# A fused gate and attention kernel: the opening written out as one straight program per engine, up to the fourth pair's turn

## The chip, the cores and the metric

The kernel runs on one core of a Trainium2 chip. The metric is the device time of one execution in microseconds (us), the median of three runs. The profile is one more execution, in which every instruction leaves a record.

## What is computed

The input x is 32 images of 64 channels of 16x16 points. Two blocks follow each other.

```
y  = mean of x over points; y = conv1d(y, w_c) over channels       # channel gate
yc = sigmoid(x * y)
sa = sigmoid(conv5x5([mean over channels of yc, max over channels of yc], w_s))   # spatial gate
x  = yc * sa + x
xn = group_norm(x, 32 groups of 2 channels) * gn_w + gn_b
q, k, v = split(qkv_w @ xn + qkv_b)         # 4 heads of 16 channels, 256 points
out = x + proj_w @ (softmax(q.T k / 4) v) + proj_b
```

All is float32. The scores are computed from q and k that are each split into three bfloat16 parts.

## The kernel before

**Pairs, units, turns.** Two images make a pair (2 x 64 channels on 128 partitions), so there are 16 pairs. A pair has eight units, one for each head of each image. The work is staged: in turn k, pair k+5 gets its spatial gate and its group statistics, k+4 is normalised (`xn`), k+3 gets queries and keys (`qk`, TensorE) and their split into three parts (GpSimd: `rest`, middle part, last part), k+2 has those parts stacked into the tiles `qs` and `ks` through DRAM, k+1 has its scores (`s`, L768) and the row maxima (`negmax`, VectorE L608), and k (from the fifth unit on) and k-1 have transposed scores (`st`, L780), exponentials (ScalarE L448) and products with the values (L794). The maxima come back into the transposed scores as one more row of `qs`: a transpose (L847), a copy (L436) and a DMA (`qs<-maxrow`, L282). Each engine runs through `turn(k, ...)`, and semaphores order the engines among each other. A wait stops all that stands behind it on its engine.

**Opening, loop and end.** Turns -5 to 2 are written out by `peeled`, turns 3 to 10 are a hardware loop over laps of four turns, turns 11 to 17 are written out again. What only the opening has (sums, maps and gates of all images, pair 0's own split) stands in between units, in dictionaries `aside` and in `beginning`:

```
peeled(range(-AHEAD, LOOP_FROM))
aside = {(-3, 6): split_0, (-2, 6): lambda: channel_gate(4), (-1, 3): lambda: channel_gate(5), (0, 3): rest_of_gates}
```

**The sync queue (SP).** Nearly all DMAs are issued by SP, in the order of its program. In a turn it issues the loads of part 0 of pair k+2, the row of maxima of pair k, the other loads of pair k+2, and the writes of the parts of pair k+3. The spatial gates of pairs 4 to 15 go through DRAM as well: `gate_write` stores a chunk, `gate_read` reads it back, spread over the channels (two DMAs for each group of four pairs, `gate<-gate_dram`). Groups 2 and 3 are read behind turns 0 and 1:

```
aside = {(-2, 1): lambda: gate_read(sp, 1), (0, 2): lambda: gate_read(sp, 2), (1, 2): lambda: gate_read(sp, 3)}
```

**Pair 0** doesn't go through DRAM: `direct` copies its parts in 12 DMAs, seven from SP and five from ScalarE's queue.

Of the kernel before, what the change touches and what calls it, by code (L numbers as in the profile page):

```python
# [16 lines left out]
F32 = mybir.dt.float32  # L17
# [5 lines left out]
P = 128  # L23
# [10 lines left out]
TERMS = ((0, 0), (1, 0), (2, 0), (0, 1), (1, 1), (0, 2))  # L34
# [3 lines left out]
BLOCKS = ((0, 1), (1, 2), (2, 4), (4, 8), (8, 12), (12, 16))  # L38
# [6 lines left out]
MAP_BANK = (0, 1, 2, 0, 2, 2, 2, 2, 2)  # L45
# [9 lines left out]
def program(nc, x, vecs, w_all, select, consts, out):  # L55
    ctx = ExitStack()
    with ctx:
# [6 lines left out]
        quad = ctx.enter_context(nc.psum_tensor("quad", [P, 4, 512], F32))  # L64
        bank = [quad[:, i, :] for i in range(4)] + [ctx.enter_context(nc.psum_tensor(f"bank{i}", [P, 512], F32)) for i in range(4, 8)]
# [79 lines left out]
        gate_in = [sem(f"gate_in{g}") for g in range(GROUPS)]  # L145
# [8 lines left out]
        split_step = sem("split_step")  # L154
        parts_out, stack_in = [sem(f"parts_out{i}") for i in range(3)], [sem(f"stack_in{r}") for r in range(RING)]
# [22 lines left out]
        AHEAD, BEHIND = 5, 2  # L178
        LOOP_FROM, LOOP_TO = 3, 11

        def stands_in(aside, k, u):

            if isinstance(k, int) and (k, u) in aside:
                aside[k, u]()

        def pipeline(eng, turn):
# [6 lines left out]
            peeled(range(-AHEAD, LOOP_FROM))  # L193
# [6 lines left out]
        def gate_write(eng, chunk, first, last, row):  # L200

            eng.wait_ge(gate_ready, chunk + 3)
            eng.dma_start(gate_dram[first:last, :], gate_s[row:row + last - first, chunk, :]).then_inc(gate_out[chunk], 16)

        def gate_read(eng, g):
            eng.wait_ge(gate_out[0 if g == 1 else 1], 16)
            for a in range(2):
                src = gate_dram[2 * g * GROUP:2 * (g + 1) * GROUP, :].rearrange("(q i) n -> i q n", i=2)[a]
                eng.dma_start(gate[C * a:C * (a + 1), g * GROUP:(g + 1) * GROUP, :],
                              src.unsqueeze(0).broadcast_to([C, GROUP, N])).then_inc(gate_in[g], 16)  # L210

# [728 lines left out]
```

## Time and profile before

| | |
|---|---|
| median of 3 runs | 183.79 us (183.75 to 183.99) |
| profiled execution: time, span of its records | 184.61 us, 182.6 us |
| TensorE busy | 163.2 us, 89% of the span |
| VectorE, ScalarE, GpSimd busy | 136.5, 121.6, 106.3 us |
| mean granted TensorE clock | 0.947 of full |

The span is from the first record to the last; times "at" something are counted from its start. PE is TensorE (PEld its weight loads), DVE VectorE, ACT ScalarE, POOL GpSimd; SPq and ACTq are the DMAs that SP and ScalarE issue. A row of a timeline has start, duration, engine, line, operation, output<-input and a count; in brackets stands how long the engine was idle before it and what ended that.

### The profile page before, as it was taken

What the parts mean: (1) busy time and instruction counts of PE and PEld (TensorE: products, weight loads), DVE (VectorE), ACT (ScalarE), POOL (GpSimd) and SP (SyncE); (2) the same over time, 40 slices, a digit from 0 to 9 for tenths busy, and PEclk for the clock granted to TensorE, in tenths of its full rate; (3) what the DMA queues carried; (4) which work ended last, traced back from release to release, by engine and by line L of the source; (5) the groups of instructions that cost most, each with busy time, mean ns of one, the idle gap of its engine ahead of it and who ended that gap; (6) DMA issues with size and microseconds to landing.
All of it is one profiled execution on the core that took longest, in us unless ns stands there. A gap on an engine that the chain in (4) does not pass through costs nothing.

```text
span 182.6 us, 4762 instructions
## 1 busy us (share of the span) xinstructions
PE 163.2 (89%) x1508; PEld 107.3 (59%) x1511; DVE 136.5 (75%) x280; ACT 121.6 (67%) x254; POOL 106.3 (58%) x206
## 2 busy tenths in 40 slices
PE   6988829999685999999999999999999999998791
PEld 3778428776451857666675766767575754553220
DVE  1567663677661889898998989899897978876433
ACT  3552343455682679887987988798797965758730
POOL 8926072681977267888888778888858350101110
PEclk9999955899997899999999999999999999999967
DMA  5940487516189544555464564564646465110001
GB/s 138 336 149 0 100 105 224 153 59 176 63 196 232 151 134 130 173 164 187 130 204 148 162 201 148 169 183 163 173 132 186 139 203 148 36 32 30 29 0 57
DMA packets 19296, 25.31 MB, mean 139 GB/s; under 512 B 3568, under 2 KB 16400, under 8 KB 19280
## 3 DMA queue, kind: packets, MB, share of 16 engines
q1 hardware_dynamic: 18560, 24.62, 46.2%
q10 hardware_dynamic: 720, 0.48, 1.6%
q8 instruction: 9, 0.15, 0.4%
q14 instruction: 7, 0.06, 0.1%
HBM read 16.22 MB, written 8.02 MB: 133 GB/s over the span
## 4 chain that ended last, share of the span: by engine, by line
PE 77%; DVE 5%; ACT 4%; POOL 4%; issue 3%; DMA 2%; ACTq 2%; SPq 2%; POOLq 0%
PE bank L794 17%; PE quad L768 16%; PE quad L780 14%; PE bank L805 7%; PE bank L824 5%; PE quad L662 5%; PE bank L815 4%; PE bank L640 2%; DMA qs<-maxrow 2%; PE bank L674 2%; ACT pt L448 2%; ACTq L217 2%; DVE negmax L608 2%; PE bank L838 1%; POOL rest L355 1%
## 5 line engine op out<-in xcount | busy, mean ns | idle before, releaser
L608 DVE TENSOR_REDUCE negmax<-quad 128x2 bf16<-128x512 f32 x128 | 83.4, 678 | 21.1 <-PE quad L768 19.4
L448 ACT ACTIVATE pt<-quad 128x512 f32<-128x512 f32 x128 | 72.8, 594 | 23.2 <-PE quad L780 23.2
L780 PE MATMUL quad<-qs,ks 97*128 97x256 bf16 x256 | 49.4, 275 | 6.7 <-ACT pt L448 3.5
L768 PE MATMUL quad<-ks,qs 96*128 96x256 bf16 x256 | 50.5, 279 | 1.2 <-DVE negmax L608 0.4
L794 PE MATMUL bank<-pt,vs 128*32 128x256 f32 x512 | 35.8, 399 | 0.0
L768 PEld LDWEIGHTS quad<-ks,qs 96*128 96x128 bf16 x256 | 21.9, 101 | 22.3 <-DVE negmax L608 13.1
L780 PEld LDWEIGHTS quad<-qs,ks 97*128 97x128 bf16 x256 | 23.8, 98 | 14.7 <-ACT pt L448 6.3
L328 POOL TENSOR_TENSOR xall<-yo,xall 128x256 f32 (+1 forms) x15 | 11.0, 731 | 31.7 <-ACT yo L472 31.7
L794 PEld LDWEIGHTS bank<-pt,vs 128*32 128x32 f32 x512 | 15.1, 112 | 12.9 <-ACT pt L448 3.3
L355 POOL TENSOR_TENSOR rest<-z,parts 128x512 f32<-128x512 f32 x15 | 17.3, 1156 | 8.0 <-issue 5.9
L805 PE MATMUL bank<-xn,wall 128*128 128x256 f32 x64 | 19.9, 397 | 0.0
L370 POOL TENSOR_TENSOR parts<-rest,parts 128x512 bf16<-128x512 f32 x15 | 17.3, 1155 | 1.5
L456 ACT ACTIVATE parts<-bank,vec 128x512 bf16<-128x512 f32 x16 | 10.8, 675 | 10.4 <-PE bank L805 7.3
L575 DVE STREAM_TRANSPOSE otok<-bank 128x512 f32<-128x512 f32 (+1 forms) x17 | 11.5, 677 | 5.9 <-PE bank L794 5.9
L440 ACT ACTIVATE xn<-xall,gnb,gna 128x256 f32<-128x256 f32 (+1 forms) x16 | 9.6, 599 | 7.4 <-POOL gnb L365 7.2
L341 POOL TENSOR_TENSOR sq<-gmv 128x1 f32<-128x1 f32 x16 | 3.1, 194 | 17.5 <-DVE gmv L561 17.4
L586 DVE STREAM_TRANSPOSE onorm<-otok 128x512 f32<-128x512 f32 (+1 forms) x17 | 11.6, 680 | 1.2 <-PE bank L824 0.6
L824 PE MATMUL bank<-onorm,wall 128*32 128x256 f32 x128 | 10.7, 406 | 1.6 <-DVE onorm L586 1.6
L662 PE MATMUL quad<-con,ycall 128*128 128x130 f32 x64 | 10.8, 321 | 0.1
L805 PEld LDWEIGHTS bank<-xn,wall 128*128 128x128 f32 x64 | 10.0, 194 | 1.1 <-issue 0.6
L335 POOL TENSOR_TENSOR ycall<-ycall,gate (+1 forms) x12 | 8.7, 726 | 3.3 <-DMA gate<-gate_dram 3.3
L815 PE MATMUL bank<-wall,xn 128*128 128x128 f32 x64 | 10.4, 287 | 0.0
(66 smaller groups left out, 207.7 us busy)
## 6 DMA issues: line engine op xcount, KB each, us to landing
parts_dram<-parts SPq DMA_DIRECT2D x45, 128.0 KB, 2.0
ks<-parts_dram SPq DMA_DIRECT2D x15, 192.0 KB, 3.0
qs<-parts_dram SPq DMA_DIRECT2D x15, 192.0 KB, 3.2
out<-xall SPq DMA_DIRECT2D x16, 128.0 KB, 2.1
qs<-parts_dram SPq DMA_DIRECT2D x15, 128.0 KB, 2.7
ks<-parts_dram SPq DMA_DIRECT2D x15, 128.0 KB, 2.8
xall<-x SPq DMA_DIRECT2D x3, 512.0 KB, 6.0
gate<-gate_dram SPq DMA_DIRECT2D x6, 256.0 KB, 4.1
```

The lines of the kernel that those rows point to most:

```text
L355: nc.gpsimd.tensor_tensor(rest[:, :], z32[:, :], parts[:, r, 0, :], ALU.subtract).then_inc(split_step, 1)
L370: nc.gpsimd.tensor_tensor(parts[:, r, 2, :], rest[:, :], parts[:, r, 1, :], ALU.subtract).then_inc(split_step, 1)
L448: nc.scalar.activation(pt[:, (u + LEAD) % UNITS, :, :].rearrange("p t n -> p (t n)"), st_bank[u % 2][:, :], ACT.Exp, scale=SCALE).then_inc ...
L586: op = nc.vector.transpose(onorm[:, cols], o_tok[:, blocks, :].rearrange("p b c -> p (b c)"))
L608: nc.vector.tensor_reduce(negmax[:, slot(1), column:column + TILES], s_bank[u % 2][:, :].rearrange("p (t n) -> p t n", t=TILES), AX.X, ALU ...
L662: mm = pe.matmul(bank[MAP_BANK[i] + p - first][:, t * (P + 2):(t + 1) * (P + 2)], ycall[:, p, t * P:(t + 1) * P], con[:, C_IDENT:C_TOEP], ...
L768: mm = pe.matmul(s_bank[u % 2][:, t * N:(t + 1) * N], qs[0:KQ, slot(1), h, a, t * P:(t + 1) * P], ks[0:KQ, slot(1), h, a, :], start=True, ...
L780: mm = pe.matmul(st_bank[u % 2][:, t * N:(t + 1) * N], ks[0:KQ + 1, slot(d), h, a, t * P:(t + 1) * P], qs[0:KQ + 1, slot(d), h, a, :], sta ...
L794: mm = pe.matmul(o_bank[32 * h:32 * h + 32, a * N:(a + 1) * N], vs[:, slot(-1), t, a, h, :], pt[:, HEADS * a + h, t, :], start=(t == 0), s ...
L805: mm = pe.matmul(z_bank[:, a * N:(a + 1) * N], w_qk[a], xn[:, slot(d), :], start=True, stop=True)
L815: mm = pe.matmul(v_psum[:, t * P:(t + 1) * P], xn[:, slot(1), t * P:(t + 1) * P], w_v, start=True, stop=True)
L824: mm = pe.matmul(y_psum[C * a + j:C * a + j + 32, :], w_p[:, j:j + 32], onorm[:, a * N:(a + 1) * N], start=True, stop=True)
```

## The change

The turns -5 to 2 are gone from `pipeline`. In their place every engine has a list of calls and waits, in an order that a search over the operations' graph gave. Turn 3 and all later ones are as before. Besides the order:

- x comes in seven blocks and not six; PSUM banks are dealt out anew (z_bank is bank 7, y_psum bank 5).
- Pair 0's queries and keys, their split and its copies go in halves (one image each). Part 0 of its keys goes through DRAM, and there are nine direct copies and one stack in place of 12 direct copies.
- Pair 0's group variance, scale and shift are computed on VectorE, except for the power.
- The gates of pairs 8 to 15 are no sigmoid on ScalarE any more, but an exponential there (`late_gates`), then a sum and a reciprocal on VectorE (`late_gate_sum`, `late_gate_reciprocal`). They come behind the switch to the exponential table. The spatial convolutions go in three chunks and not two.
- The rows of maxima of pairs 0, 1 and 2 are issued by ScalarE; from pair 3 on SP does it.

```diff
-BLOCKS = ((0, 1), (1, 2), (2, 4), (4, 8), (8, 12), (12, 16))
+BLOCKS = ((0, 1), (1, 2), (2, 4), (4, 6), (6, 8), (8, 12), (12, 16))
...
-            peeled(range(-AHEAD, LOOP_FROM))
...
+            sp.wait_ge(split_step, 12)
+            part_write(2, 0)
+            sp.wait_ge(gate_ready, 5)
+            late_gate_write(sp)
+            sp.wait_ge(parts_out[1], 64)
+            stack(qs, 0, 3, 2, 0)
+            stack(ks, 1, 3, 2, 0, part=1)
+            sp.wait_ge(parts_out[2], 64)
+            stack(qs, 0, 0, 3, 0)
+            stack(ks, 1, 5, 1, 0, part=2)
+            sp.wait_ge(gate_out[1], 16)
+            gate_read(sp, 2, 0)
+            gate_read(sp, 2, 1)
+            sp.wait_ge(late_gate_in, 32)
+            gate_read(sp, 3, 0)
+            gate_read(sp, 3, 1)
+            sp.wait_ge(p1_ready, 5)
+            part_write(0, 1)
+            sp.wait_ge(split_step, 14)
+            part_write(1, 1)
+            sp.wait_ge(split_step, 15)
+            part_write(2, 1)
...
+            def late_gates():
+                nc.scalar.activation(gate_s[0:4 * GROUP, 0, :], chunk_bank[2][0:4 * GROUP, 0:N], ACT.Exp, scale=-1.0).then_inc(dexp_ready, 1)
...
+            exponentials(3)
+            late_gates()
...
+            dve.wait_ge(s_ready, 26)
+            maximum(3, 1)
+            dve.wait_ge(gs_ready, 7)
+            group_moments()
+            norm_reciprocal()
+            dve.wait_ge(gn_stat, 15)
+            aggregate()
+            late_gate_reciprocal()
+            maximum(3, 2)
```

In the calls, `maximum(p, u)`, `scores(p, u)` and `scores_t(p, u)` are unit u of pair p. The wait for `parts_out[2]` at 64 is for the last part of pair 4.

**SP, from the writes of pair 4's parts to the loop.** Before, from turn 1: the last three lines of a turn, the reads of group 3, and turn 2 with pair 4's loads (`qs<-parts_dram`, `ks<-parts_dram`) around pair 2's row of maxima:

```order
L261 DMA parts_dram<-parts 128x512 x3
L209 DMA gate<-gate_dram 64x4x256 x2
L257 DMA ks<-parts_dram 48x1x2048
L257 DMA qs<-parts_dram 16x2048
L282 DMA qs<-maxrow 1x16x128
L257 DMA qs<-parts_dram 32x1x2048
L257 DMA ks<-parts_dram 32x1x2048
L257 DMA qs<-parts_dram 48x1x2048
L257 DMA ks<-parts_dram 16x2048
L261 DMA parts_dram<-parts 128x512 x3
```

The changed kernel at the same place; the three writes are pair 5's parts, and the first two loads behind the branch and the row of maxima are turn 3's (pair 5, pair 3):

```order
L251 DMA parts_dram<-parts 128x512
L201 DMA gate_dram<-gate_s 16x256
L248 DMA qs<-parts_dram 32x1x2048
L248 DMA ks<-parts_dram 32x1x2048
L248 DMA qs<-parts_dram 48x1x2048
L248 DMA ks<-parts_dram 16x2048
L205 DMA gate<-gate_dram 64x4x256 x4
L251 DMA parts_dram<-parts 128x512 x3
L191 UNCONDITIONAL_BRANCH
L191 ISA
L248 DMA ks<-parts_dram 48x1x2048
L248 DMA qs<-parts_dram 16x2048
```

All four reads of late gates moved behind the loads of pair 4 and ahead of the writes of pair 5's parts, which before stood two turns behind the first of these reads; the row of maxima of pair 3 is the next DMA behind the last row shown.

**VectorE, the first pair.** Before, from the first block's sums to the first pair's statistics (`ysum<-xall` are channel sums, `maps` the channel maximum and mean, `ycall<-ycall,gate` the first gating):

```order
L482 TENSOR_REDUCE ysum<-xall 128x2
L490 TENSOR_REDUCE maps<-quad 128x2x2
L493 COPY maps<-quad 128x2x2
L490 TENSOR_REDUCE maps<-quad 128x2x2
L493 COPY maps<-quad 128x2x2
L482 TENSOR_REDUCE ysum<-xall 128x4
L500 TENSOR_TENSOR ycall<-ycall,gate 128x256
```

And in the changed kernel:

```order
L885 TENSOR_REDUCE maps<-quad 128x2x2
L891 COPY maps<-quad 128x2x2
L876 TENSOR_REDUCE ysum<-xall 128x2 x2
L885 TENSOR_REDUCE maps<-quad 128x2x2
L891 COPY maps<-quad 128x2x2
L876 TENSOR_REDUCE ysum<-xall 128x2
L876 TENSOR_REDUCE ysum<-xall 128x4
L896 TENSOR_TENSOR ycall<-ycall,gate 128x256
```

The sums of pairs 8 to 11 (`128x4`), whose x is loaded behind the weights `wall`, now stand ahead of the first gating.

**ScalarE, the late gates.** Before, the sigmoid of the late chunk, its DMA and the table switch stand ahead of the first exponential (`pt<-quad`):

```order
L397 ACTIVATE gate_s<-bank 16x256
L203 DMA gate_dram<-gate_s 16x256
L426 ACT_TABLE_LOAD
L426 ACTIVATE junk<-mhalf 128x1
L448 ACTIVATE pt<-quad 128x512
```

In the changed kernel:

```order
L623 ACT_TABLE_LOAD
L623 ACTIVATE junk<-mhalf 128x1
L667 ACTIVATE pt<-quad 128x512 x4
L642 ACTIVATE gate_s<-quad 16x256
L667 ACTIVATE pt<-quad 128x512
```

The late chunk's operation moved behind four exponentials.

## Rows read from the trace of the kernel before

**Rows 1.** Busy time by stage; the columns are named in the first line.
```profile
core 0: us, PE busy (x) PEld busy (x) DVE busy (x) ACT busy (x) POOL busy (x), PEclk, DMA share, GB/s
0.00:28.34 28.34, 21.56 (x123) 15.72 (x124) 15.55 (x39) 12.06 (x29) 16.78 (x34) 0.91 0.53 134
28.34:39.50 11.16, 10.81 (x58) 8.31 (x58) 7.42 (x15) 4.70 (x11) 6.12 (x14) 0.77 0.57 165
39.50:50.15 10.65, 8.72 (x63) 6.30 (x65) 7.00 (x17) 6.39 (x12) 6.33 (x13) 1.00 0.39 116
50.15:62.90 12.75, 9.71 (x82) 6.12 (x81) 6.57 (x13) 6.71 (x14) 7.20 (x16) 0.87 0.84 206
62.90:70.85 7.95, 7.95 (x87) 5.53 (x86) 7.37 (x16) 6.71 (x15) 5.37 (x10) 1.00 0.39 118
70.85:78.80 7.95, 7.95 (x87) 5.48 (x86) 7.37 (x16) 6.84 (x15) 6.65 (x14) 1.00 0.56 169
```

**Rows 2.** Timeline: TensorE's stall in the opening, and its units in turn 3.
```profile
57.01 0.38 PE L780 MATMUL quad<-qs,ks 97*128 97x256 bf16 x2 [3.04 <-DMA qs<-maxrow]
...
74.08 0.38 PE L780 MATMUL quad<-qs,ks 97*128 97x256 bf16 x2
...
77.95 0.38 PE L768 MATMUL quad<-ks,qs 96*128 96x256 bf16 x2
```

**Rows 3.** Timeline of the opening's first part, pair 0.
```profile
4.62 0.51 SPq L238 DMA_DIRECT2D wall<-w_all  x1
8.22 1.22 DVE L482 TENSOR_REDUCE ysum<-xall 128x4 f32<-128x1024 f32 x1
10.52 0.42 DVE L500 TENSOR_TENSOR ycall<-ycall,gate 128x256 f32<-128x256 f32 x1 [1.08 <-ACT gate L393]
15.28 0.60 ACT L440 ACTIVATE xn<-xall,gnb,gna 128x256 f32<-128x256 f32 x1 [1.72 <-POOL gnb L365]
18.43 0.69 SPq L217 DMA_DIRECT2D qs<-parts  x1
```

**Rows 4.** Source line L238 (the weights): time from issue to landing.
```profile
DMA to landing us min/median/max: 6.1/6.1/6.1
```

**Rows 5.** Source line L217 (pair 0's direct copies): from issue to landing.
```profile
DMA to landing us min/median/max: 2.7/3.6/4.4
```

**Rows 6.** Costliest groups, from the page: busy, mean ns, idle before.
```profile
L608 DVE TENSOR_REDUCE negmax<-quad 128x2 bf16<-128x512 f32 x128 | 83.4, 678 | 21.1 <-PE quad L768 19.4
L448 ACT ACTIVATE pt<-quad 128x512 f32<-128x512 f32 x128 | 72.8, 594 | 23.2 <-PE quad L780 23.2
L456 ACT ACTIVATE parts<-bank,vec 128x512 bf16<-128x512 f32 x16 | 10.8, 675 | 10.4 <-PE bank L805 7.3
L440 ACT ACTIVATE xn<-xall,gnb,gna 128x256 f32<-128x256 f32 (+1 forms) x16 | 9.6, 599 | 7.4 <-POOL gnb L365 7.2
```

**Rows 7.** Timeline of ScalarE: table switch, first exponentials, values.
```profile
44.30 1.28 ACT L426 ACT_TABLE_LOAD   x1 [0.41 <-ACT gate_s L397]
45.70 0.58 ACT L448 ACTIVATE pt<-quad 128x512 f32<-128x512 f32 x1
48.44 1.66 ACT L448 ACTIVATE pt<-quad 128x512 f32<-128x512 f32 x3
53.17 0.34 ACT L465 COPY vs<-bank 128x256 f32<-128x256 f32 x1
```

**Rows 8.** Source line L209 (reads of spread gates): issue time, landing.
```profile
L209 SPq DMA_DIRECT2D gate<-gate_dram x6: 617/620/653, 26.9 to 57.9; - x6
...
DMA to landing us min/median/max: 3.7/4.1/4.6
```

**Rows 9.** Source line L261 (writes of parts), 28 to 28.7 us, behind gate reads.
```profile
DMA to landing us min/median/max: 3.6/3.6/3.6
```

**Rows 10.** The same line L261 over the whole span.
```profile
DMA to landing us min/median/max: 1.7/2.0/4.4
```

**Rows 11.** Source line L257 (loads of stacked parts): ns of issue, landing.
```profile
L257 SPq DMA_DIRECT2D qs<-parts_dram x45: 541/588/1587, 30.0 to 152.8; - x45
...
DMA to landing us min/median/max: 2.5/3.0/4.6
```

**Rows 12.** Source line L282 (rows of maxima) over the whole span.
```profile
DMA to landing us min/median/max: 1.7/2.4/4.2
```

**Rows 13.** Chain that ended last: units at half and at full clock.
```profile
59.79 0.43 PE quad L780 x2
...
63.42 0.22 PE quad L780 x2
```

More of the change, by code:

```diff
@@ new lines, in _, with stack @@
+            load_x(6)
+            def stack(tile, g, first, count, r, part=None):
+                rows = slice(first * HD, (first + count) * HD)
+                if part is None:
+                    src = parts_dram[r, 0:count, g, :, :].rearrange("s d n -> d s n")
+                else:
+                    src = parts_dram[r, part, g, :, :].unsqueeze(1).broadcast_to([HD, count, HEADS * 2 * N])
+                sp.dma_start(tile[rows, r, :, :, :].rearrange("p h a n -> p (h a n)"), src).then_inc(stack_in[r], 16)
@@ L280, in turn @@
+            part_write(2, 1)
+            def turn(k, slot, has, lap):
+                if has(2):
+                    wait(sp, parts_out[0], 16 * (k + 3))
+                    stack(ks, 1, 0, 3, slot(2), part=0)
+                    stack(qs, 0, 5, 1, slot(2))
                 if has(0):
                     wait(sp, mrow_ready, k + 1)
[L282 to L283 removed]
@@ L290, in turn @@
+                if has(3):
+                    wait(sp, p1_ready, k + 3)
+                    part_write(0, slot(3))
                 if has(-3):
@@ L610, in turn @@
                                                 AX.X, ALU.max, negate=True).then_inc(max_done, 1)
-                    if u == 7 and has(5) and not late:
+                    if u == 7 and has(5):
                         gn_group()
@@ L615, in turn @@
                             norm(i, -2, 1 if last(-2) else None)
-                    if u == 3 and has(5) and not late:
+                    if u == 3 and has(5):
                         gn_stats(0)
-                    if u == 4 and has(5) and not late:
+                    if u == 4 and has(5):
                         gn_stats(1)
@@ new lines, in _ @@
+            pe.wait_ge(max_done, 2)
+            scores(0, 3)
+            values(0)
+            pe.wait_ge(max_done, 3)
+            scores(0, 4)
+            keep_busy(1, bank[5])
+            pe.wait_ge(max_done, 4)
+            scores(0, 5)
+            keep_busy(2, bank[5])
+            pe.wait_ge(max_done, 5)
+            scores(0, 6)
+            keep_busy(1, bank[5])
+            pe.wait_ge(max_done, 6)
+            scores(0, 7)
+            pe.wait_ge(yc_ready, 16)
+            transposes(8)
@@ new lines, in _ @@
+            scores_t(2, 0)
+            pe.wait_ge(exp_done, 16)
+            scores_t(2, 1)
+            pe.wait_ge(max_done, 28)
+            scores(3, 5)
+            products(1, 1)
+            pe.wait_ge(exp_done, 17)
+            scores_t(2, 2)
+            pe.wait_ge(max_done, 29)
+            scores(3, 6)
+            pe.wait_ge(exp_done, 18)
+            scores_t(2, 3)
+            queries_keys(6 % RING, 0)
+            pe.wait_ge(norm_step, 4)
+            projection()
+            values(3)
@@ L862, in turn @@
                         maxt()
-                    if u == 0 and has(3) and not first_turns:
+                    if u == 0 and has(3):
                         qk(1, 3)
```

1243 lines of the change are left out of this document (955 added, 288 removed).

## The prediction

> **What bounds the kernel now.** I read the busy time by stage first, then the chain that ended last, then timelines of the opening. From turn 3 on, a turn takes 7.95 us with TensorE busy throughout and VectorE 7.37 us of it [rows 1]; that part is not touched, so the change is worth what it moves the start of a turn behind the opening. The opening takes 70.85 us to the first maximum of pair 4. The reader should see four poor stages in it [rows 1]: 28.34 us until pair 0's scores; 11.16 us for pair 0; 10.65 us for pair 1; 12.75 us for pair 2, with 3.04 us in which TensorE waits for a row of maxima to land [rows 2]. Only pair 3 runs at the loop's pace. VectorE is busy 43.9 us of the 70.85 (15.55, 7.42, 7.00, 6.57 and 7.37), so 27 us are idle on the engine that limits the loop with TensorE. That is the room for another order.
>
> I use as yardstick the transposed scores of unit 0 of pair 3, the fifth unit of turn 3: they start at 74.08 us, and turn 4's scores 3.87 us later, at 77.95 [rows 2]. What follows is the same code in both kernels, at the same pace.
>
> **The change, part by part.**
>
> *Up to pair 0's scores: no gain.* The first gating on VectorE, at 10.52 us, now stands behind the sums of pairs 8 to 11 (1.22 us [rows 3]). Their x is loaded behind `wall`, and the bytes up to its end are those that before ended with `wall`, at 4.62 + 6.1 = 10.7 us [rows 3, 4]. So the gating comes at 10.7 + 1.2 = 11.9 or 12.0 us, 1.5 later. From there to `xn` of pair 0 it took 4.8 us [rows 3]. The steps computed on VectorE save two hops to GpSimd, but they queue behind a gating, maps, statistics and a residual of pair 1, so I take 5.2 us: `xn` at 17.2, 1.9 later. Pair 0's halves save the wait for the other half: ScalarE has `xn` 0.6, a spatial gate 0.4, three channel gates 1.4 and two half first parts 0.8, so the first copies go at 20.4 instead of 18.43 us [rows 3]. Behind that come two half middle parts 0.8, `xn` 0.6, two copies 1.3, first part and `z32` of pair 1 1.4, a scale and a gate 0.6: the last copy goes from ScalarE's queue at 25.1. With 2.7 to 4.4 us to land [rows 5], I take 3.3: scores at 28.4 us, as before (28.34). The bounds are 27 and 30.
>
> *Pairs 0 and 1.* Less TensorE and VectorE work stands between pair 0's units, since the maps of pairs 8 to 11 go ahead of them. VectorE has eight maxima at 0.68 [rows 6] and about 1.3 us of other work, 6.7 us; the granted clock was 0.77 over this stage [rows 1], half speed for its first 5 us, and TensorE idles again ahead of it, so I add 2 us: pair 0 ends at 37.2, not 39.5. Pair 1's stack waits on SP for the landing of the gate write, then for two gate reads: complete at 37.8 by my count of the queue, 36.9 before; its scores start there. ScalarE then has `z32` of pair 3, the values, the first part of pair 3 (0.7, 0.34, 0.68 [rows 6, 7]) and the table switch with its dummy (1.4 from start to the first exponential [rows 7]): first exponential at 37.8 + 1.1 for the scores and the projection that feed it, + 1.7 + 1.5 = 42.1 us, where before it was at 45.70 [rows 7]. That is 3.6 us gained.
>
> *Until the late gates are done.* The next thing that matters is the reciprocal of the late gates, since SP waits for it. Ahead of it ScalarE has twelve exponentials (0.53 each in a row, 1.66 for three [rows 7]; 6.4 with two odd ones), `late_gates` 0.4, two rows of maxima 0.5, the issue of one 0.55, values 0.35, two `xn` 1.2, first part and `z32` of pair 4 1.35: 10.9 us, so 53.0. TensorE then has the queries and keys of pair 5 and the group statistics (1.6), and VectorE moments, two short steps and the reciprocal: 2.0 in all, gates done at G = 55.0 us. If it all ran without one wait it would be G = 53; before, four exponentials from 45.70 took until 50.1 where 2.1 would do [rows 7], so 57 or 58 is as possible.
>
> *Loop entry.* ScalarE needs another 5.4 us for eight exponentials and what stands between, and pair 4's loads land at G + 6.3: pair 4's first maximum comes at about 61.5 us, not 70.85. Nine microseconds are gained there.
>
> *The tail on SP takes most back.* Behind G, SP issues in order: the write of the gates (0.4), four loads of pair 4 (0.59 each [rows 11], and half a microsecond of wait for pair 4's last part: 2.9), then the reads of group 2. It waits for these to land before it reads group 3 (one issue 0.65 and the median with the second read, 4.35: 5.0 [rows 8]), issues the two reads of group 3 (1.3), the writes of pair 5's parts, waits for the first to land (3.6, as behind two gate reads before [rows 9]), issues two loads (1.2), and only then the row of maxima of pair 3, which takes 2.5 us [rows 12]. Sum: 0.4 + 2.9 + 5.0 + 1.3 + 3.6 + 1.2 + 2.5 = 16.9 us, so the row is there at 71.9 and the yardstick runs at 72.0. Without that wait it would run about 4.5 us behind the loop entry, at 66. So TensorE stands for 6 us in the middle of turn 3, and VectorE and ScalarE with it; GpSimd and SP catch up meanwhile. The yardstick is 2.1 us earlier than 74.08.
>
> *The clock.* Before, behind a stall of 3.04 us, units ran at 0.43 us each instead of 0.22 [rows 2, 13]. A longer stall should do the same to the last four scores and four transposed ones: 8 x 0.21 = 1.7 us at most, nothing if VectorE's 0.68 per maximum hides it. I take half, 0.8.
>
> **Sum.** 2.1 - 0.8 = 1.3 us less. The profiled execution took 184.61 us (span 182.6), the median is 183.79; I apply the difference to the median: 182.5 us. Before and after differ in measurement by about 0.2% (0.37 us) at no change.
>
> The row of maxima of pairs 0 to 2 moves to ScalarE's queue. It landed 4.2 us after issue behind two gate reads on the same queue as against a median of 2.4 [rows 12]. The Trainium skill, page "DMA: Bandwidth & Descriptors", section "Issuing engines are not separate DMA queues", says that DMAs of all issuers interleave on the same 16 DMA engines and another issuer saves only the time to initiate. By that the move saves what SP would have spent ahead of it and no landing time. My sum has no gain in landing for it.
>
> **The rivals.**
>
> *The tail is short (B).* If every DMA of the tail takes its shortest time seen, the reads take 0.65 + 3.7, the part 1.7 and the row 1.7 [rows 8, 10, 12], and pair 4's last part is no wait (2.4): 0.4 + 2.4 + 4.35 + 1.3 + 1.7 + 1.2 + 1.7 = 13.05 us. The yardstick is at 68.1, 6.0 us earlier, the clock takes 0.5: 178.3 us. For it: fewer DMAs are under way then than in the loop's own turns. Against it: all six gate reads took 3.7 to 4.6 us, in three different places. The skill's same page, section "Anatomy of one DMA", gives a fixed cost of about 2.0 us and bytes at 436 GB/s for GpSimd's path, which would be an estimated 2.6 us for a 256 KB read; rows 8 show 3.7 as the least, so the trace does not agree for these reads, whose source is broadcast.
>
> *The gates come late (C), slower.* The tail hangs on G alone. It decides from G = 74.08 - 17.0 - 0.8 = 56.3 us on. If the opening's chain through ScalarE meets as many gaps as before (exponentials at half their pace while TensorE, in order, waits for maxima), G is 58.0 and the yardstick at 75.0 + 0.8, so 185.5 us. For it: every step above was counted nearly without gaps, and TensorE's list mixes scores that wait for VectorE with transposed scores that wait for ScalarE, two banks each. Against it: pair 3 already ran such a mix at the loop's pace before [rows 1].
>
> *The order is right and nothing is given back (D).* The row of maxima would have to be issued in time although it stands last on SP: 183.8 - 9.3 = 174.5 us. Only if the late gates were done before pair 3's scores; VectorE's list has them behind its second maximum. It is the far end of B.
>
> **How the numbers follow.** A, the forecast with G between 53.5 and 56.7: 0.53, its own range 181.0 to 184.2. B with D: 0.22, 174.5 to 180.5. C: 0.25, 184.2 to 187. Faster by over 0.2% is below 183.4: 0.43 of A and all of B, 0.65. Same: 0.08, from A. Slower: 0.02 of A and C, 0.27. The range from 176.0 to 186.0 leaves out the ends of B and C, 2 in 10.
>
> **What would show it.** First exponential near 42, and pair 4's first maximum near 61 to 62 us. In turn 3 the transposed scores of pair 3 wait some 6 us for `qs<-maxrow`, whose issue on SP comes about 14 us behind the reciprocal, behind four gate reads. The clock at half behind it. The prediction is wrong if pair 0's scores start more than 1.5 us ahead of 28.3, if G is far from 55, or if SP gets to the row of maxima by the time that turn 3 starts.

## The result, and the profile after

| | before | after |
|---|---|---|
| median | 183.89 us (183.75 to 188.39, 4 runs) | 191.01 us (189.09 to 199.16, 4 runs) |
| profiled execution: time, span | 184.61, 182.6 us | 189.09, 186.9 us |
| mean granted clock | 0.947 | 0.954 |

The changed kernel is slower: the ratio is 1.0355, with a 95% interval of 1.0254 to 1.0456. Some executions of either kernel fall into a slower state and take some per cent longer, so ratios here and below leave them out, while medians keep them. The prediction (182.5 us, 176.0 to 186.0) was wrong in sign and range; the rival of late gates (C) came true in its mechanism, and the time lies beyond its 187 us as well. The profiled execution is the shortest of the four, so the traces explain 4.5 us; that the others took 1.6 to 10.1 us more is not in them.

The busy time by stage. The cuts are pair 0's scores (27.14), pair 1's scores (37.85), the end of the late chunk's convolution (46.8), the transpose of pair 2's maxima (57.25), pair 4's first maximum (67.76) and turn 4's first scores (83.20), each to within 0.3 us. They aren't all the events of [rows 1], so only the first stage and the last are to be compared with it, and those roughly:

```profile
core 0: us, PE busy (x) PEld busy (x) DVE busy (x) ACT busy (x) POOL busy (x), PEclk, DMA share, GB/s
0.00:27.10 27.10, 24.12 (x147) 17.23 (x147) 17.45 (x49) 13.62 (x36) 14.70 (x27) 1.00 0.47 149
27.10:37.85 10.75, 7.74 (x52) 5.40 (x53) 7.02 (x15) 3.77 (x8) 7.25 (x15) 0.96 0.59 159
37.85:46.80 8.95, 8.95 (x36) 5.62 (x37) 4.54 (x8) 4.22 (x7) 6.79 (x12) 0.50 0.54 144
46.80:57.00 10.20, 9.64 (x92) 6.54 (x92) 7.88 (x15) 7.67 (x17) 3.70 (x12) 0.98 0.33 88
57.00:67.70 10.70, 9.78 (x93) 5.99 (x91) 9.72 (x19) 7.81 (x16) 8.29 (x14) 1.00 0.58 149
67.70:83.40 15.70, 9.62 (x83) 5.75 (x84) 7.24 (x15) 6.54 (x14) 6.64 (x14) 0.78 0.52 150
```

The last stage is turn 3. Before, a turn took 7.95 us with TensorE busy throughout; now turn 3 takes 16.2 us from its first scores to turn 4's (67.02 to 83.20), and TensorE is busy for 9.62 us of the 15.70 shown. Pair 1's stage is the other poor one: TensorE is busy all of its 8.95 us, but with 36 matmuls at half clock, and VectorE and ScalarE are busy half the time. The timeline of the changed kernel, along the path that matters:

```profile
16.12 0.60 ACT L645 ACTIVATE xn<-xall,gnb,gna 128x256 f32<-128x256 f32 x1
...
27.14 0.61 PE L1302 MATMUL quad<-ks,qs 96*128 96x256 bf16 x4 [1.22 <-DMA ks<-parts_dram]
...
37.85 0.61 PE L1302 MATMUL quad<-ks,qs 96*128 96x256 bf16 x2 [1.11 <-DMA ks<-parts_dram]
...
43.49 1.09 ACT L667 ACTIVATE pt<-quad 128x512 f32<-128x512 f32 x2 [0.38 <-PE quad L1309]
...
44.18 2.64 PE L1265 MATMUL quad<-con,maps 128*16 128x256 f32 x8
...
47.61 1.08 ACT L667 ACTIVATE pt<-quad 128x512 f32<-128x512 f32 x2 [3.03 <-PE quad L1309]
...
55.87 0.69 ACT L657 ACTIVATE z<-bank,vec 128x512 f32<-128x512 f32 x1
...
56.72 1.22 DVE L935 TENSOR_SCALAR gate_s<-gate_s 16x256 f32<-16x256 f32 x1
...
59.86 1.70 DVE L938 RECIPROCAL gate_s<-gate_s 16x256 f32<-16x256 f32 x1
...
61.59 0.32 SPq L201 DMA_DIRECT2D gate_dram<-gate_s  x1
...
64.44 5.89 SPq L205 DMA_DIRECT2D gate<-gate_dram  x4
70.37 1.61 SPq L251 DMA_DIRECT2D parts_dram<-parts  x3
...
75.36 0.57 SPq L215 DMA_DIRECT2D qs<-maxrow  x1
...
77.58 0.61 PE L1575 MATMUL quad<-qs,ks 97*128 97x256 bf16 x2 [5.79 <-DMA qs<-maxrow]
...
83.20 0.38 PE L1563 MATMUL quad<-ks,qs 96*128 96x256 bf16 x2
```

The reader should see three things. The late gates are done at 59.86 + 1.70 = 61.56 us. From there SP does 13.8 us of issues and waits before it comes to the row of maxima at 75.36. TensorE stands for 5.79 us, and the yardstick runs at 77.58 us, where it was at 74.08 [rows 2]. Turn 4's scores follow 5.62 us later, not 3.87. So turn 4 is 5.25 us late (83.20 against 77.95), but the span is only 4.3 us longer. From turn 4 to the end the changed kernel takes 103.7 us and the kernel before 104.65, although the code is the same: before, the clock stood at 0.78 of full from 170 to 182 us, and in the changed kernel at 1.00 from 170 to 182.

### The profile page after: what moved, and what is told of

Read it like the earlier page. It is cut to its first block, busy times and chain, and to the rows that moved or that the text cites. A ratio compares the mean times of both kernels' runs of the same rounds, so it can differ in the third digit from the quotient of the medians.

```text
span 186.9 us, 4721 instructions
## 1 busy us (share of the span) xinstructions
PE 165.8 (89%) x1519; PEld 106.4 (57%) x1519; DVE 139.8 (75%) x289; ACT 122.1 (65%) x258; POOL 105.9 (57%) x200
## 4 chain that ended last, share of the span: by engine, by line
PE 60%; DMA 15%; SPq 9%; DVE 8%; ACT 4%; issue 2%
PE quad L1589 14%; PE quad L1563 12%; PE quad L1575 12%; PE quad L1617 5%; DMA parts_dram<-parts 5%; PE bank L1598 4%; DMA xall<-x 3%; SPq L248 3%; PE bank L1608 3%; DMA qs<-maxrow 3%; DMA gate<-gate_dram 2%; PE quad L1265 2%; PE quad L1302 2%; ACT pt L847 2%; SPq L210 2%
## 5 line engine op out<-in xcount | busy, mean ns | idle before, releaser
L1575 PE MATMUL quad<-qs,ks 97*128 97x256 bf16 x216 | 41.4, 274 | 8.3 <-DMA qs<-maxrow 5.8
L573 POOL TENSOR_TENSOR xall<-yo,xall 128x256 f32 (+1 forms) x15 | 10.9, 730 | 37.5 <-ACT yo L867 36.0
L1589 PE MATMUL quad<-pt,vs 128*32 128x256 f32 x448 | 30.6, 392 | 0.1
L1575 PEld LDWEIGHTS quad<-qs,ks 97*128 97x128 bf16 x216 | 19.8, 98 | 15.1 <-DMA qs<-maxrow 6.1
L1563 PEld LDWEIGHTS quad<-ks,qs 96*128 96x128 bf16 x192 | 15.8, 100 | 16.7 <-DVE negmax L1211 10.9
L1589 PEld LDWEIGHTS quad<-pt,vs 128*32 128x32 f32 x448 | 13.1, 111 | 11.4 <-ACT pt L847 2.8
L1190 DVE STREAM_TRANSPOSE otok<-quad 128x512 f32<-128x512 f32 (+1 forms) x15 | 10.1, 672 | 5.3 <-PE quad L1589 5.3
L1598 PE MATMUL bank<-xn,wall 128*128 128x256 f32 x38 | 11.8, 393 | 0.0
L1617 PE MATMUL quad<-onorm,wall 128*32 128x256 f32 x120 | 10.0, 407 | 1.6 <-DVE onorm L1201 1.6
L1201 DVE STREAM_TRANSPOSE onorm<-otok 128x512 f32<-128x512 f32 (+1 forms) x16 | 10.9, 678 | 0.5
L1253 PE MATMUL quad<-con,ycall 128*128 128x130 f32 x64 | 10.0, 304 | 0.1
L1253 PEld LDWEIGHTS quad<-con,ycall 128*128 128x128 f32 x64 | 8.6, 208 | 1.9 <-ACT ycall L633 0.7
```

The source lines that it names most:

```text
L1253: mm = pe.matmul(bank[MAP_BANK[i] + p - first][:, t * (P + 2):(t + 1) * (P + 2)], ycall[:, p, t * P:(t + 1) * P], con[:, C_IDENT:C_TOEP], ...
L1563: mm = pe.matmul(s_bank[u % 2][:, t * N:(t + 1) * N], qs[0:KQ, slot(1), h, a, t * P:(t + 1) * P], ks[0:KQ, slot(1), h, a, :], start=True, ...
L1575: mm = pe.matmul(st_bank[u % 2][:, t * N:(t + 1) * N], ks[0:KQ + 1, slot(d), h, a, t * P:(t + 1) * P], qs[0:KQ + 1, slot(d), h, a, :], sta ...
L1589: mm = pe.matmul(o_bank[32 * h:32 * h + 32, a * N:(a + 1) * N], vs[:, slot(-1), t, a, h, :], pt[:, HEADS * a + h, t, :], start=(t == 0), s ...
L1598: mm = pe.matmul(z_bank[:, a * N:(a + 1) * N], w_qk[a], xn[:, slot(d), :], start=True, stop=True)
L1617: mm = pe.matmul(y_psum[C * a + j:C * a + j + 32, :], w_p[:, j:j + 32], onorm[:, a * N:(a + 1) * N], start=True, stop=True)
```

## The experiments

Each run below stands beside runs of the kernel before on the same chip: its medians were 185.18 us (the first four), 184.43 (the next four) and 185.54 (the last four). The changed kernel itself was not run again on those chips, so a ratio beside its 1.0355, or beside one of another group of four, may compare two chips. "Yardstick" is the transposed scores of unit 0 of pair 3, "turn 4" the first scores of turn 4; both, and TensorE's longest idle time in turn 3, are of the profiled execution.

| kernel | median us | ratio to before, interval | gates written | turn 3 starts | longest idle | yardstick | turn 4 |
|---|---|---|---|---|---|---|---|
| before | | | | 70.00 | 0 | 74.08 | 77.95 |
| after | 191.01 | 1.0355, 1.0254 to 1.0456 | 61.59 | 67.02 | 5.79 | 77.58 | 83.20 |
| e1 | 188.49 | 1.0105, 1.0041 to 1.0169 | 61.9 | 67.49 | 4.67 | 76.75 | 82.97 |
| e2 | 190.2 | 1.0253, 1.0188 to 1.0319 | 65.45 | 66.89 | 2.42 | 74.04 | 79.54 |
| e3 | 191.0 | 1.0337, 1.0282 to 1.0391 | 59.33 | 65.32 | 6.83 | 76.40 | 83.71 |
| e4 | 187.74 | none on record | 57.12 | 62.93 | 6.78 | 74.10 | 80.37 |
| e5 | 182.72 | 0.9914, 0.9872 to 0.9956 | 44.20 | 66.00 | 2.54 | 71.70 | 75.57 |
| e6 | 187.21 | 1.0184, 1.009 to 1.0279 | 57.60 | 63.39 | 6.45 | 74.25 | 79.78 |
| e7 | 180.82 | 0.9832, 0.9759 to 0.9906 | 43.60 | 65.86 | 3.07 | 71.54 | 75.41 |
| e8 | 196.26 | 1.0656, 1.0578 to 1.0734 | 61.34 | 66.98 | 4.73 | 71.89 | 81.36 |
| e9 | 189.75 | 1.0137, 1.0093 to 1.0181 | 46.4 | 66.20 | 7.24 | 77.70 | 84.01 |
| e10 | 187.29 | 1.0098, 1.004 to 1.0156 | 46.9 | 72.06 | 4.96 | 78.03 | 82.27 |
| e11 | 183.1 | 0.9825, 0.9756 to 0.9895 | 47.0 | 68.48 | 2.33 | 72.57 | 77.34 |
| e12 | 180.65 | 0.9634, 0.9584 to 0.9684 | 43.3 | 65.72 | 0.76 | 69.81 | 74.86 |

**e1: the reads of groups 2 and 3 without the wait between them.**

```diff
-.then_inc(gate_in if g == 1 else late_gate_in, 16)
+.then_inc((gate_in, late_gate_in, last_gate_in)[g - 1], 16)
...
-            sp.wait_ge(late_gate_in, 32)
```

> The changed kernel, but SP doesn't wait for the gates of group 2 to land before it reads group 3: each group has a semaphore of its own. All else is as in the changed kernel (median 191.0 us, profiled 189.1). Theory 'SP tail' (the row of maxima of pair 3 is late because SP gets to it late): the wait of 4.0 us goes, the reads of group 3 and what stands behind them come 4 us earlier, perhaps 1 us of it lost to slower landings; TensorE's stall in turn 3 shrinks from 5.8 to about 3 us and the median falls to 187 to 188.5. Rival 'DMA engines are full' (the row is late because the bytes ahead of it are, whoever waits): the reads and the writes behind them land later by as much, the stall stays at 5 us or more, median 190 to 191. Rival 'clock': the stall plays no part beside TensorE's half clock from 37 to 47 us; no change.

The sync queue's timeline of this kernel:

```profile
65.12 2.58 SPq L205 DMA_DIRECT2D gate<-gate_dram  x4
67.75 1.59 SPq L251 DMA_DIRECT2D parts_dram<-parts  x3
72.89 0.57 SPq L248 DMA_DIRECT2D ks<-parts_dram  x1
...
74.23 0.57 SPq L215 DMA_DIRECT2D qs<-maxrow  x1
```

The four reads take 2.58 us of SP and not 5.89. But the write of pair 5's part behind them is now only known to have landed 5.1 us after its issue (67.75 to 72.89), where it was 3.65 (70.37 to 74.02). With reads that began 0.7 us later, the row goes out only 1.1 us earlier. Four 256 KB reads in a row are in the way of what comes behind them, whether SP waits or not. By the ratio much more was won than the trace shows: 1.0105, where the changed kernel has 1.0355 and e3, on the same chip as this run, 1.0337. Turn 4 is only 0.23 us earlier, but the profiled execution took 189.48 us, and four of the ten took 184.9 to 187.1; what those gained is in no trace. So the wait costs time, and without it the kernel is still 1% slower than before.

**e2: SP's order.** Gates written and group 2 read behind the writes of pair 5's parts, SP's turn 3 at once, group 3 behind it.

```diff
             part_write(2, 1)
+            sp.wait_ge(gate_out[1], 16)
+            gate_read(sp, 2, 0)
+            gate_read(sp, 2, 1)
...
+            if behind_3:
+                peeled([LOOP_FROM])
+                behind_3()
```

> The changed kernel with another order on SP alone: the late gates are written and group 2 read behind pair 5's writes; turn 3 of SP follows at once (loads of pair 5, row of maxima of pair 3), and group 3 is read behind turn 3. No DMA is added or removed. Theory 'SP tail': the stall of 5.8 us in turn 3 goes and with it the half clock behind it; the transposed scores of pair 3 start near 72 us and not at 77.6, turn 4 near 76.5 and not at 83.4; median 184 (7 less), a profiled time of 182 to 184. If the tail only moves (the gates of pair 8 land too late for GpSimd instead), a stall of 2 to 4 us stays and the median is 186 to 188. Rival 'clock in pair 1': no more than 1 us less than 191.

The stall of turn 3 shrinks to 2.42 us and turn 4 starts 3.7 us earlier than in the changed kernel. Then it comes back, on TensorE's timeline:

```profile
74.04 0.61 PE L1581 MATMUL quad<-qs,ks 97*128 97x256 bf16 x2 [2.42 <-DMA qs<-maxrow]
...
86.48 0.39 PE L1581 MATMUL quad<-qs,ks 97*128 97x256 bf16 x2 [2.71 <-DMA qs<-maxrow]
```

GpSimd waits 5.25 us for the gates of group 2 (until 72.79), the parts of later pairs are late, and the median is that of the changed kernel within 1 us. Neither of the two places tried for the reads is free when the gates come at 61 us.

**e3: the late gates as a sigmoid ahead of the table switch**, with the convolution behind the first pair's maxima on TensorE and no sum and reciprocal on VectorE. SP's order is unchanged.

```diff
+            act.wait_ge(sconv_ready, 5)
+            late_gates()
             exp_table()
...
-            late_gate_sum()
...
-            late_gate_reciprocal()
```

> The changed kernel, but the late gates are again a sigmoid on ScalarE ahead of the table switch, with their convolution behind pair 0's maxima in place of one filling matmul; sum and reciprocal on VectorE (1.22 and 1.70 us in the trace) are gone. SP's order is untouched, so its tail with the four reads stays. Theory 'late gates' (what I mis-sized is the way to the gates): SP no longer waits for the reciprocal (61.56 us) but only for pair 4's last part (59.8, itself perhaps 1 to 2 us earlier since the convolution of 2.6 us no longer stands between pair 1's scores); the tail begins 2 to 4 us earlier and the median falls by as much, to 187 to 189, with the stall still there (5 to 8 us, the loop being entered earlier as well). Theory 'SP tail only': the stall gets longer by what the loop entry gains, and the median falls by no more than 1.7 us. If the convolution in its new place holds up pair 1 (its scores start at 37.85), 1 us is lost of that.

The gates are ready early, but SP comes to their write only at 59.33 us, since it stands behind pair 4's last part. On SP and TensorE:

```profile
58.86 0.42 SPq L251 DMA_DIRECT2D parts_dram<-parts  x1
59.33 0.43 SPq L201 DMA_DIRECT2D gate_dram<-gate_s  x1
...
76.40 0.61 PE L1574 MATMUL quad<-qs,ks 97*128 97x256 bf16 x2 [6.83 <-DMA qs<-maxrow]
```

Turn 3 starts 1.7 us earlier and TensorE comes to the stall 2.2 us earlier (69.57 against 71.79), but the row is earlier by only 1.2 us, so the stall is 1.0 us longer. Behind it the clock takes the rest: turn 4 starts 0.5 us later than in the changed kernel, and the ratio, 1.0337, isn't apart from 1.0355. Without sum and reciprocal nothing is won as long as SP's order stays.

**e4: the sums of pairs 8 to 11 behind pair 0's statistics on VectorE.**

```diff
-            ysums(5)
...
             aggregate()
+            dve.wait_ge(x_in[5], 16)
+            ysums(5)
```

> The changed kernel with one call moved on VectorE: the channel sums of pairs 8 to 11, which wait for x to land until 10.7 us, stand behind pair 0's statistics and not ahead of its first gating (TensorE's convolution of these sums waits for them). My claim in the prediction: these sums delay pair 0 by over a microsecond. If so, the first gating starts near 10.3 instead of 11.9 us and xn of pair 0 0.8 to 1.5 us ahead of 16.1. Whether the kernel gets faster by it depends on what holds pair 1: if it is pair 0's way, the median falls by 0.5 to 1.2 us; if it is the gates' way through DRAM (pair 1's stack complete at 37.8 us), the stack comes earlier only as far as the chunk's gate does, and the median falls by less than 0.5, which these runs may not tell.

The first gating comes at 9.24 us and not 11.82, pair 0's scores at 25.88. The clock is not at half between pair 1's scores this time, and the late chunk's convolution takes half as long:

```profile
39.80 1.42 PE L1265 MATMUL quad<-con,maps 128*16 128x256 f32 x8
...
74.10 0.61 PE L1576 MATMUL quad<-qs,ks 97*128 97x256 bf16 x2 [6.78 <-DMA qs<-maxrow]
```

The gates are written 4.5 us earlier, and the yardstick moves 3.5 us. So the yardstick moves with the gates, as the prediction's tail has it. It is then at the time of before, but turn 4 comes 6.27 us behind it: the clock falls in the stall, at 72.4 us, and stays at half to 79.2. What the move is worth in time isn't settled: two of its four executions took 185.04 and 187.48 us, and no ratio was formed.

**e5: gates early, and read in SP's gap.** The sigmoid of e3, the write ahead of pair 3's loads, all four reads behind them (at 50 us, when SP waits for pair 4's first part), and a semaphore for each group.

```diff
+            sp.wait_ge(gate_ready, 5)
+            late_gate_write(sp)
             sp.wait_ge(parts_out[0], 64)
             stack(ks, 1, 0, 3, 3, part=0)
...
             stack(ks, 1, 5, 1, 3, part=2)
+            sp.wait_ge(gate_out[1], 16)
+            gate_read(sp, 2, 0)
+            gate_read(sp, 2, 1)
+            gate_read(sp, 3, 0)
+            gate_read(sp, 3, 1)
```

> The changed kernel with the late gates as a sigmoid ahead of the table switch (as in e3), and with their write on SP behind the third part of pair 3 is written and part 0 of it waited for (near 44 us), all four reads behind pair 3's loads (near 50 us), where SP waited 6 us for pair 4's first part; each group has its own semaphore. SP's list behind pair 4's loads then has only pair 5's writes. Theory 'late gates make SP late': the stall of 5.8 to 6.8 us in turn 3 goes altogether, the loop is entered near 66 us and pair 5's first maximum is near 74 us, where the changed kernel has 84.0; ratio to the kernel before 0.97 to 0.985. Rival 'bytes': the reads only push the loads and rows of pairs 2 to 4 back, and 2 to 4 us of stall turn up in turns 1 and 2; ratio 0.99 to 1.01.

The long stall is gone, and the kernel is 0.9% faster than before (0.4 to 1.3%):

```profile
50.06 2.58 SPq L205 DMA_DIRECT2D gate<-gate_dram  x4
...
66.00 0.39 PE L1562 MATMUL quad<-ks,qs 96*128 96x256 bf16 x2 [2.54 <-DMA ks<-parts_dram]
...
67.46 0.55 SPq L215 DMA_DIRECT2D qs<-maxrow  x1
```

The row of maxima goes out 1.5 us behind the start of turn 3. What TensorE waits for now, 2.54 us, is pair 4's stack: its first part, issued right behind the four reads at 53.42, took 4.0 us to land. The ratio, 0.9914, is in the range of the rival "bytes" (0.99 to 1.01) and above that of the theory (0.97 to 0.985). So the theory is right about the stall and the rival in part about the price.

**e6: nine more filling matmuls ahead of pair 1's scores and between its units**, nothing else.

```diff
             transposes(8)
+            keep_busy(6, bank[2])
...
-            keep_busy(1, bank[2])
+            keep_busy(4, bank[2])
```

> The changed kernel with nine more filling multiplications on TensorE (0.22 us each at full clock) in its idle time ahead of pair 1's scores: six behind the last transposes, three more behind pair 0's transposed maxima. Their results aren't used. Theory 'clock': the granted clock at half from 37.2 to 47.4 us is what the idle TensorE from 33.7 to 37.8 us brings; with the filling it stays full, pair 2's first maximum comes 3 to 4 us earlier than 48.9, the late gates' end as well, and the ratio falls from 1.0355 to about 1.012 to 1.02 with the stall in turn 3 still there. If the clock falls all the same, the ratio stays at 1.03 to 1.04.

The granted clock in 40 slices of the span, from the page of the changed kernel:

```profile
PEclk9999999955999999579999999999999999999999
```

And from the page of this one:

```profile
PEclk9999999999999997599999999999999999999999
```

The first fall is gone, the late gates are written at 57.60 us, and turn 4 starts 3.4 us earlier. So the clock at half in pair 1's stage was worth about 4 us of the gates' lateness, and in this execution work for an idle TensorE was enough to keep it up. The stall of 6.45 us and the second fall are still there.

**e7: e5 and the moved sums of e4.**

```diff
-            ysums(5)
...
+            ysums(5)
...
+            pe.wait_ge(ysum_ready, 6)
             channel_conv(5)
```

> e5 and the moved sums of e4 together. If both theories hold, what each gives adds up: loop entry near 64 us or earlier (e4 had 64.5 with the late gates still on VectorE), no stall in turn 3, pair 5's first maximum near 72 us where the kernel before has 78.8: ratio 0.955 to 0.97, the only one of these kernels clearly faster than before. If the loop entry is bounded by another thing (the loads of pairs 2 and 3 through SP), pair 5 comes at 74 to 76 us and the ratio is 0.975 to 0.99.

It has the edits of both and no other. The median is 1.9 us below that of e5, beside the same runs of before. In the profiled execution hardly any of it is left in the opening (turn 4 0.16 us earlier), and the intervals of the ratios overlap: that the sums add to e5 is likely, not shown.

**e8: all rows of maxima issued by ScalarE, in the loop too.**

```diff
-                if has(0):
-                    wait(sp, mrow_ready, k + 1)
-                    row_of_maxima(sp, k, slot(0))
...
+                        wait(act, mrow_ready, k + 1)
+                        row_of_maxima(act, k, slot(0))
```

> The changed kernel, but all rows of maxima in the loop and behind it are issued by ScalarE too (0.55 us of its queue in each turn), not by SP. Theory 'the row stands last on SP': the transposed scores of pair 3 don't wait, but pair 5's loads are as late as before (last one issued near 78.9, landing near 82), so that turn 4 can't start before 82 us: the stall of 5.8 us moves from the middle of turn 3 to its end and shrinks by 1 to 2 us; ratio 1.02 to 1.03. If instead the row alone was late and all else is in time, pair 5's first maximum comes at 76 to 77 us and the ratio is 0.99 to 1.00. Against both stands a cost in every turn if ScalarE's queue holds up its exponentials: a longer turn than 7.95 us.

The row of pair 3 is in time: the yardstick runs at 71.89 us, without a stall. But the next thing on SP behind the gate reads is pair 5's stack, and TensorE stands for that instead:

```profile
81.36 0.59 PE L1562 MATMUL quad<-ks,qs 96*128 96x256 bf16 x2 [4.73 <-DMA ks<-parts_dram]
```

And the loop pays for the issue on ScalarE: by VectorE's timeline the first maxima of pairs 8 and 12 are 33.7 us apart, 8.42 us a turn, where before they are 31.8 apart, 7.95 a turn. From turn 4 to the end this kernel takes 111.7 us and the changed one 103.7. Of these 8.0 us, 12 x 0.46 = 5.5 go to the turns; most of the rest is turn 4 itself, 10.6 us, at half clock until 88 us. Since turn 4 starts 1.8 us earlier, the span is 6.2 us longer (193.1 against 186.9).

**e9: gates early, but the reads where the changed kernel has them** (e5 without its moved reads and without the semaphores).

```diff
+            sp.wait_ge(gate_ready, 5)
+            late_gate_write(sp)
             sp.wait_ge(parts_out[0], 64)
```

> The late gates are computed as a sigmoid before the table switch and written to DRAM at about 44 us, but their four reads stay behind pair 4's loads, with the wait between the groups. Theory 'place on SP': the reads are issued from 63.3 us on, take 6 us with the wait, and the row of maxima of pair 3 is issued near 74 us, where it was 67.5 with the reads in the gap; TensorE stands about 5 to 6 us in turn 3, and the median is 187 to 190. Rival 'lateness alone': what cost time was that gates written at 61.6 us held up the queue; with the write at 44 the rest is hidden, the stall is under 2 us and the median is 182 to 184.

```profile
63.84 6.06 SPq L205 DMA_DIRECT2D gate<-gate_dram  x4
...
77.70 0.60 PE L1574 MATMUL quad<-qs,ks 97*128 97x256 bf16 x2 [7.24 <-DMA qs<-maxrow]
```

The gates are in DRAM 17 us before they are read, and the stall is the longest of all. It came out as "place on SP" said. Early gates alone don't bring the kernel level with before. That its ratio, 1.0137, is 2% below that of the changed kernel isn't explained by this trace, whose yardstick is no earlier (77.70 against 77.58); its opening also lost 2 us that e5's didn't (last section).

**e10: e5 with the wait between the groups kept.**

```diff
+            gate_read(sp, 2, 0)
+            gate_read(sp, 2, 1)
+            sp.wait_ge(late_gate_in, 32)
+            gate_read(sp, 3, 0)
+            gate_read(sp, 3, 1)
```

> As the kernel with the reads in SP's gap (182.7), but with the one semaphore and the wait of group 3 for group 2's landing, as in the changed kernel. Theory 'place on SP': the wait of some 4 us falls where SP waits for pair 4's parts anyway (3 us of the gap are free), so pair 4's first part is written up to 3 us later and loop entry slips by 0 to 2 us: 182.5 to 185. Rival 'the wait between the reads': the wait is what costs, wherever it stands: 186 or more.

The measured 187.29 us is what the rival said. The gap is some 3.6 us long (e11's part goes out 3.56 us behind the start of its reads) and the reads with the wait need 6:

```profile
52.61 5.94 SPq L205 DMA_DIRECT2D gate<-gate_dram  x4
...
58.60 0.61 SPq L251 DMA_DIRECT2D parts_dram<-parts  x1
...
72.06 0.61 PE L1562 MATMUL quad<-ks,qs 96*128 96x256 bf16 x2 [4.96 <-DMA ks<-parts_dram]
```

Pair 4's first part is written 2.4 us later than in e11 (56.17 us), whose reads also start at 52.61, and turn 3 starts 3.6 us later. I had taken the gap for wide enough. Both parts of e5's edit on SP are needed: the place and the parted semaphores. e11, on the same chip, differs from e10 by its filling too; e5, which doesn't, ran on another, and its interval (0.9872 to 0.9956) is apart from that of e10 as well.

**e11: e5 with six more filling matmuls** (the first edit of e6; the text below says five).

```diff
+            keep_busy(6, bank[2])
             pe.wait_ge(xn_ready, 4)
```

> As the kernel with the reads in SP's gap (182.7), with five more filling matmuls of 128x512 on TensorE ahead of pair 1's scores. Theory 'the clock in the opening costs': the granted clock is not at half from 37 to 41 us, the late convolution takes 1.4 us and not 2.4, pair 4's first maximum comes 1 to 2 us earlier: 181 to 182. Rival 'pair 4 waits for the chain through ScalarE and GpSimd': the clock is full there, but pair 4's loads land at the same time, and the median stays within 0.3% of 182.7.

The clock is full from 36 to 46 us, as expected. But the median is that of e5 within 0.2%, the ratio is not apart from that of e5 (0.9914 and 0.9825, the intervals overlap), and the two ran on different chips. It stays open.

**e12: e7 with the same filling.**

```diff
+            keep_busy(6, bank[2])
             pe.wait_ge(xn_ready, 4)
```

> As the kernel with moved sums and reads in the gap (180.8), with the same filling. Theory 'clock': 179 to 180.3. Rival: within 0.3% of 180.8.

The fastest kernel of the study. By the medians, 180.65 beside 185.54 us, it is 2.6% faster than before, by the ratio 3.7% (3.2 to 4.2%). That ratio rests on two of its four executions, 178.71 and 179.49 us; the shorter one had a mean granted clock of 1.000. The profiled one took 181.8 us, and in it the clock still fell (0.72 from 44 to 56 us). TensorE waits no longer than 1.02 us for anything in turns 3 and 4. Its interval doesn't touch that of e7, but the chips differ, so what the filling is worth on top of e7 isn't settled.

## Why the prediction was wrong

**The step that failed is "Until the late gates are done": G = 55.0 us, measured 61.56.** The 6.56 us come from three of its terms. The sum was nearly one without waits (its items of ScalarE add up to 10.75, not 10.9), so the 53 us that I named as the bound without any wait lies below what the sum itself gives.

- *The first exponential*, 42.1 us, came at 43.49: 1.4 us. Pair 1's scores started at 37.85 as forecast (37.8), but at half clock.
- *ScalarE's work without gaps.* From the first exponential to the end of `z32` of pair 4 I had 10.9 us; it took 13.07 (43.49 to 56.56), 2.2 more. Most of it is one gap of 3.03 us, in which TensorE did the late chunk's convolution: 2.64 us at half clock, 1.42 at full clock in e4. My sum for this stage had neither the convolution's place between pair 1's scores nor a clock at half. In e3, where the convolution stands elsewhere, the same stretch took 10.25 us (44.32 to 54.57). e6 shows what the half clock was worth in this term and the one before it: with filling the gates are written 4.0 us earlier.
- *"Moments, two short steps and the reciprocal: 2.0 in all"* took 5.0 (56.56 to 61.56). The reciprocal alone took 1.70, and I had priced it within the 2.0 without a row for it. A maximum, a transpose and statistics stand around it, and the sum `TENSOR_SCALAR` took 1.22 us. This term alone isn't what made the kernel slow: e3 has neither sum nor reciprocal, its gates are written 2.3 us earlier, behind pair 4's last part, and its ratio is the same.

I gave G = 57 or 58 as possible, and rival C 0.25; G lay beyond that too.

**The tail on SP was right.** From G to the yardstick it took 77.58 - 61.56 = 16.0 us, forecast 16.9: reads 5.93 us against 5.0 + 1.3, the landing of pair 5's part 3.65 against 3.6, the row 2.2 against 2.5. TensorE's stall was 5.79 us, forecast 6; both its ends came about 6 us late. With G as measured my own sum gives 61.56 + 16.9 = 78.5, 4.4 us behind 74.08, plus 0.8: 189.8 us against the profiled 184.61, where 189.09 was measured. That it comes so near is in part luck: the clock cost more than 0.8 us, and the end, which I had taken as equal, gave 0.95 us back. Rival C's bound, G = 56.3, was about right: in e4 and e6, with gates at 57.1 and 57.6, the yardsticks are at 74.10 and 74.25, level with 74.08, and their turn 4 is still 2.4 and 1.8 us late.

**The clock was undersized.** I took 0.8 us, at most 1.7. Between the yardstick and turn 4 the changed kernel loses 5.62 - 3.87 = 1.75 us, e1, e4 and e9 lose 2.3 to 2.4, e3 3.4. In the changed kernel it is at half from 74.5 to 81.4 us: it falls in the stall, and products and projections behind it run at half speed besides the scores that I had counted.

**The opening.** Pair 0's `xn` came at 16.12 us, not 17.2, and its scores at 27.14, not 28.4: the queue on VectorE cost less than I had given it; which of the steps saved it wasn't tested. Turn 3 started at 67.02 us and not near 61; that follows from G.

**Another issuer saves no landing time, but more than the time to initiate.** In e8 the rows, from ScalarE, land after a median of 2.8 us, in the changed kernel after 2.4. But pair 3's row is issued at 68.28 us and not at 75.36, since it no longer stands behind SP's waits, and the loop pays for it with 0.46 us a turn. The Trainium skill, page "DMA: Bandwidth & Descriptors", section "Issuing engines are not separate DMA queues", has another issuer save only the time to initiate. The trace agrees as far as landing goes; where the first issuer stands in waits, these 7.1 us are far more than that.

**Where the gain went.** Shown by e5, e9 and e10: with the gates as a sigmoid the new opening beats the old one by 0.4 to 1.3% (e5) as soon as the reads of late gates don't stand, with their wait, between the last loads of pair 4 and pair 5's parts on SP. In the changed kernel they do, and place and wait together cost more than the order gains; e1 shows that the wait is a part of it and not all. Not shown is how much of the changed kernel's distance in the medians is variation between executions. I had taken that for 0.2%, which no row shows: the runs of before that enter the first group's ratios alone lie between 182.94 and 185.26 us.

## What to carry to other kernels

Cost the operation on which a whole queue waits from a row for its own form, and if there is none give it a wide bound: here a reciprocal on 16 partitions, priced without a row, headed 16 us of serial DMA work. When an order is made anew, look for the one queue with a long chain behind a late value and ask two things: can the value be made earlier, and is there idle time of that queue to put its use in; e9 and e10 show that the early value without the idle place, or with the wait kept in it, still leaves the kernel 1% or more behind the one before. A long stall of TensorE cost its length and then 1.7 to 3.4 us at half clock here, so count the units behind it too, and where it idles ahead of critical work, try filling it.

## What the hardware showed that I had not expected

- VectorE's reciprocal of 16x256 float32 took 1.70 us in all six traces that have it (after, e1, e2, e4, e6, e8), while a maximum over 128x512 takes 0.68. The exponential or the sigmoid of the same 16x256 tile on ScalarE took 0.36 (L642).
- Adding a constant to the same tile took VectorE 1.22 us. It ended 0.15 us behind GpSimd's 1.16 us `rest<-z,parts`, which had started 0.09 us before it. In e6 it started 0.18 us behind, took 1.12 us and again ended 0.14 us behind. That one held the other up fits both traces, but wasn't tested.
- One and the same program can meet the clock differently. e5 and e9 are alike on all engines up to pair 0's scores; in e9 TensorE had 0.56 us of work between 12 and 14 us and the clock fell behind it, in e5 1.49 us and it didn't. Pair 0's scores came at 29.19 us and at 27.11. e5 had no more work, it had it later: e9 did the first 16 matmuls of the spatial convolution in 1.47 us and e5 in 2.52 (the clock's column says 1.00 in both), and both then had to wait for the same step on VectorE, in e9 for 2.04 us and in e5 for 0.51. So the execution that was faster at first was the later one in the end. TensorE at that step, of e9 and of e5:

```profile
13.44 0.38 PE L1286 MATMUL bank<-mv,con 128*128 128x2 f32 x2 [2.04 <-DVE mv L906]
```

```profile
13.44 0.38 PE L1286 MATMUL bank<-mv,con 128*128 128x2 f32 x2 [0.51 <-DVE mv L906]
```

  The busy time in three windows, of e9:

```profile
12.00:14.00 2.00, 0.56 (x5) 0.56 (x6) 1.90 (x6) 0.00 (x0) 0.00 (x0) 1.00 0.00 0
14.00:16.00 2.00, 2.00 (x11) 1.14 (x11) 1.93 (x11) 1.66 (x6) 0.61 (x1) 0.66 0.00 0
16.00:18.00 2.00, 2.00 (x9) 1.34 (x7) 1.22 (x2) 1.77 (x5) 0.00 (x0) 0.50 0.00 0
```

  And of e5:

```profile
12.00:14.00 2.00, 1.49 (x16) 1.28 (x15) 1.90 (x6) 0.85 (x3) 0.00 (x0) 1.00 0.00 0
14.00:16.00 2.00, 2.00 (x15) 1.25 (x15) 1.93 (x11) 1.67 (x6) 0.61 (x1) 1.00 0.04 8
16.00:18.00 2.00, 2.00 (x17) 1.95 (x17) 1.92 (x5) 1.90 (x6) 0.39 (x3) 1.00 0.00 0
```
